# Causal attention in blocks of 256 queries instead of 512, taken from the longest to the shortest, with one exponential over four heads

## The reference

```
scores = (q @ k.T) * 16 ** -0.5            # 1536 x 1536, keys after the query masked out
probs  = exp(scores - max(scores)) / sum    # over the keys
ctx    = probs @ v                          # 1536 x 16
```

## Time and profile before

| | us |
|---|---|
| median of 3 runs (5064.18 to 5069.74) | 5069.07 |
| the profiled execution | 5058.97 |
| its span, first to last instruction | 5056.8 |
| busy: TensorE | 4046.9 (80%) |
| busy: VectorE | 2799.3 (55%) |
| busy: ScalarE | 2255.8 (45%) |
| busy: GpSimd | 494.5 (10%) |
| mean granted clock of TensorE | 0.882 |

### The profile page before, as it was taken

How to read it: one execution, slowest core, us unless ns; L and a number is a source line. 1 busy time by engine, 2 the same in 40 slices (tenths; PEclk the granted TensorE clock), 3 DMA queues, 4 the chain that set the end, 5 groups by cost and what they waited for, 6 DMA issues and landing times. The chain is left out here.

```text
span 5056.8 us, 70418 instructions
## 1 busy us (share of the span) xinstructions
PE 4046.9 (80%) x26656; PEld 2691.9 (53%) x26656; DVE 2799.3 (55%) x6139; ACT 2255.8 (45%) x3803; POOL 494.5 (10%) x824
## 2 busy tenths in 40 slices
PE   6786866799887876799887775799887876799888
PEld 4664644465546544365546554365546554365546
DVE  4555737355555738355555648455545747455544
ACT  3343648254342548254342558254342549244332
POOL 0000010201100010201100010201100010201100
PEclk9898977899898987899898887899898987899988
DMA  2000000000000000000000000000000000000000
GB/s 89 3 3 17 1 17 1 1 1 1 1 1 4 1 17 1 0 1 1 1 1 4 1 18 1 0 1 1 1 1 4 1 1 1 1 1 1 1 1 4
DMA packets 28313, 26.52 MB, mean 5 GB/s; under 512 B 10550, under 2 KB 26934, under 8 KB 27450
## 3 DMA queue, kind: packets, MB, share of 16 engines
q1 hardware_dynamic: 27962, 21.98, 1.5%
HBM read 20.40 MB, written 1.57 MB: 4 GB/s over the span
## 5 line engine op out<-in xcount | busy, mean ns | idle before, releaser
L720 ACT ACTIVATE big<-ps,negmax 128x1024 f32<-128x1024 f32 (+1 forms) x672 | 600.1, 899 | 266.1 <-DVE negmax L753 266.0
L706 ACT COPY big<-ps 128x512 f32<-128x512 f32 x672 | 394.1, 586 | 493.2 <-PE ps L647 490.1
L753 DVE TENSOR_REDUCE negmax<-ps 128x1 f32<-128x1536 f32 x336 | 589.9, 1758 | 38.2 <-PE ps L623 18.5
L647 PE MATMUL ps<-cst,big 128*128 128x128 f32 x4032 | 502.7, 275 | 30.4 <-ACT big L720 29.9
L647 PEld LDWEIGHTS ps<-cst,big 128*128 128x128 f32 x4032 | 457.2, 142 | 48.5 <-ACT big L720 40.5
L424 PE MATMUL ps<-cst 128*128 128x512 f32 x608 | 310.0, 666 | 128.4 <-DVEq L190 58.2
L437 ACT COPY xt<-ps 64x512 f32<-64x512 f32 x144 | 78.9, 579 | 710.7 <-PE ps L429 710.6
L616 PE MATMUL ps<-kup,qup 128*128 128x512 f32 (+3 forms) x768 | 359.2, 565 | 41.8 <-POOLq L190 41.0
L409 POOL TENSOR_TENSOR st<-st,cst 128x6 f32<-128x6 f32 x104 | 156.8, 1508 | 2187.1 <-DVE st L397 2183.0
L663 PE MATMUL ps<-big,v 128*32 128x128 f32 (+1 forms) x8064 | 321.9, 277 | 8.1 <-DVE ctxt L1244 6.0
L616 PE MATMUL ps<-klo,qlo 128*128 128x512 f32 (+3 forms) x672 | 313.7, 550 | 3.6 <-DVE big L706 1.6
(11 more groups left out here) (394 smaller groups left out, 7239.0 us busy)
## 6 DMA issues: line engine op xcount, KB each, us to landing
rw<-in_w_route SPq DMA_DIRECT2D x128, 64.5 KB, 1.8
cst<-in_consts SPq DMA_DIRECT2D x1, 2671.0 KB, 14.6
cst<-in_consts SPq DMA_DIRECT2D x1, 2670.5 KB, 8.7
big<-in_consts SPq DMA_DIRECT2D x1, 1872.5 KB, 21.7
out_dram<-res SPq DMA_DIRECT2D x4, 384.0 KB, 2.9
experts_in<-in_consts SPq DMA_DIRECT2D x1, 1360.0 KB, 17.4
qup<-in_patches SPq DMA_DIRECT2D x4, 260.0 KB
klo<-in_pe_low SPq DMA_DIRECT2D x2, 384.0 KB, 23.1
```

What stands on the lines that cost most here:

```text
L647: ins = nc.tensor.transpose(turned_bank(kind, u, g)[:, i * P:(i + 1) * P], prob[:, slot_of(kind, u), (4 * g + i) * P:(4 * g + i + 1) * P], ...
L706: copy(pt[:, slot_of(kind, u), g, 0:n], turned_bank(kind, u, g)[:, 0:n]).then_inc(*ph.mark(copier(kind, g)))
L720: nc.scalar.activation(prob[:, slot_of(kind, u), cols], src[:, cols], ACT.Exp, bias=bias, accum_out=part_sum[:, u, k:k + 1]).then_inc(*ph. ...
L753: nc.vector.tensor_reduce(negmax[:, u:u + 1], flat[:, 0:n], AX.X, ALU.max, negate=True)\
```

## The change

The blocks become 256 queries (two tiles), and there are six, in the order `seq4` = 5, 4, 3, 2, 1, 0, so the first has 12 steps and the last 2. `cross` now does all four heads of a key tile in one go, four matmuls of 256 columns into two banks, each followed by its edge, and one exponential takes all four (four buffers of `weight` as before, each now one step). The two opening parts of the block after next come before the shifts of the next (`first_parts`); these parts, the shifts and the shift rows are taken before the last exponential and the last two value steps of a block, and the last value step, the copy of the sums and the turn back go into the next block. The shift rows are all copied by ScalarE, four of 256; `keep_clock` goes from four to two. Bank 4 is split: shifts in one half, turned sums in the other. `sums` has two halves by turns.

```diff
-        def steps4(jb):
-            return 4 * (jb + 1)
+        seq4 = (5, 4, 3, 2, 1, 0)
+        half4 = 2 * P
+        def steps4(p):
+            return 2 * (seq4[p] + 1)
...
+            def cross(p, kt):
...
+                edge = kt >= 2 * seq4[p]
+                for hd in range(HEADS):
+                    at = half4 * (hd % 2) + off
+                    bank = ps[:, 2 * (m % 2) + hd // 2, :]
+                    ins = nc.tensor.matmul(bank[:, at:at + half4 - off], k4(hd // 2)[:, kt * P:(kt + 1) * P].bitcast(F32R),
+                                           q4(hd)[:, half4 * seq4[p] + off:half4 * (seq4[p] + 1)].bitcast(F32R),
+                                           start=True, stop=not edge, skip_group_check=True)
+                    if edge:
+                        ins = nc.tensor.matmul(bank[:, at:at + P], future_b[:, :], ident_b[:, :], start=False, stop=True,
+                                               skip_group_check=True)
...
             for i in range(len(parts4(0))):
                 part(0, i)
-            keep_clock(7, 4)
+            keep_clock(7, 2)
+            first_parts(1)
             shifts(0)
...
+            for p in range(len(seq4)):
+                rest = len(parts4(p + 1)) - 2 if p + 1 < len(seq4) else 0
+                for kt in range(steps4(p)):
+                    cross(p, kt)
+                    begin, end = 2 + rest * kt // steps4(p), 2 + rest * (kt + 1) // steps4(p)
+                    middle = (begin + end) // 2
+                    for i in range(begin, middle):
+                        part(p + 1, i)
+                    if kt == steps4(p) - 1 and p + 1 < len(seq4):
+                        for i in range(middle, end):
+                            part(p + 1, i)
+                        first_parts(p + 2)
+                        shifts(p + 1)
                     if kt > 0:
-                        weigh(jb, kt - 1)
...
+                        weigh(p, kt - 1)
+                    elif p > 0:
+                        weigh(p - 1, steps4(p - 1) - 1)
+                    if kt == 1 and p > 0:
+                        turn_back(p - 1)
...
+            def shift_rows(p):
+                act.wait_ge(*ph.after("shift_psum", p + 1))
+                for hd in range(HEADS):
+                    nc.scalar.copy(q4(hd)[64:66, half4 * seq4[p]:half4 * (seq4[p] + 1)].bitcast(F32R),
+                                   ps[32 * hd:32 * hd + 2, 4, 0:half4]).then_inc(*ph.mark("shift_by_act"))
...
+            for p in range(len(seq4)):
+                for kt in range(steps4(p)):
+                    if kt == steps4(p) - 1 and p + 1 < len(seq4):
+                        shift_rows(p + 1)
...
-                for hd in (2, 3):
-                    nc.vector.tensor_copy(q4(hd)[64:66, 512 * jb:512 * (jb + 1)].bitcast(F32R), ps[32 * hd:32 * hd + 2, 4, :])\
-                        .then_inc(*ph.mark("shift_by_vec"))
```

More of the change, by code:

```diff
@@ L1094, in part, with shifts @@
                 ins.then_inc(*ph.mark("part_ready"))
[L1096 to L1111 removed]
+            def shifts(p):
+                pe.wait_ge(*ph.after("shift_ready", p + 1))
+                if p >= 1:
+                    pe.wait_ge(*ph.after("shift_by_act", HEADS * p))
+                for i in range(2):
+                    ins = nc.tensor.matmul(ps[:, 4, i * P:(i + 1) * P], shift[:, i, :], ident, start=True, stop=True,
+                                           skip_group_check=True)
+                ins.then_inc(*ph.mark("shift_psum"))
@@ L1112, in cross @@
+            def cross(p, kt):
+                m = cross_before(p) + kt
+                off = reach(p, kt)
+                if kt == 0:
+                    pe.wait_ge(*ph.after("shift_by_act", HEADS * (p + 1)))
                 if m >= 2:
                     pe.wait_ge(*ph.after("cross_done", m - 1))
-                edge = kt >= 4 * jb
-                for i in range(2):
-                    bank = ps[:, 2 * (m % 2) + i, :]
-                    ins = nc.tensor.matmul(bank[:, off:512], k4(g)[:, kt * P:(kt + 1) * P].bitcast(F32R),
-                                           q4(2 * g + i)[:, 512 * jb + off:512 * (jb + 1)].bitcast(F32R),
-                                           start=True, stop=not edge, skip_group_check=True)
@@ L1120, in cross @@
-                for i in range(2 if edge else 0):
-                    bank = ps[:, 2 * (m % 2) + i, :]
-                    ins = nc.tensor.matmul(bank[:, off:off + P], future_b[:, :], ident_b[:, :], start=False, stop=True,
-                                           skip_group_check=True)
-                ins.then_inc(*ph.mark("cross_psum"))
-            def weigh(jb, kt):
-                m = cross_before(jb) + 2 * kt
-                off = reach(jb, kt)
-                if kt == 0 and jb >= 1:
-                    pe.wait_ge(*ph.after("sums_copied", jb))
-                pe.wait_ge(*ph.after("cross_done", m + 2))
-                for hd in range(HEADS):
-                    ins = nc.tensor.matmul(ps[32 * hd:32 * hd + 32, 7, off:512], v4[:, kt, hd // 2, :],
-                                           weight[:, 2 * (m % 4) + hd, off:512], start=(kt == 0), stop=(kt == steps4(jb) - 1))
-                if kt == steps4(jb) - 1:
-                    ins.then_inc(*ph.mark("sums_ready"))
@@ new lines, in cross, with weigh @@
+                ins.then_inc(*ph.mark("cross_psum"))
+            def weigh(p, kt):
+                m = cross_before(p) + kt
+                off = reach(p, kt)
+                if kt == 0 and p >= 1:
+                    pe.wait_ge(*ph.after("sums_copied", p))
+                pe.wait_ge(*ph.after("cross_done", m + 1))
+                for hd in range(HEADS):
+                    ins = nc.tensor.matmul(ps[32 * hd:32 * hd + 32, 7, off:half4], v4[:, kt, hd // 2, :],
+                                           weight[:, m % 4, hd, off:half4], start=(kt == 0), stop=(kt == steps4(p) - 1),
+                                           skip_group_check=True)
+                if kt == steps4(p) - 1:
+                    ins.then_inc(*ph.mark("sums_ready"))
@@ new lines, in causal_pe @@
+            for p in range(len(seq4)):
[11 more added lines that the diff above has]
+                        shifts(p + 1)
+                    if kt > 0:
+                        weigh(p, kt - 1)
[3 more added lines that the diff above has]
+                        turn_back(p - 1)
+                    if kt < steps4(p) - 1:
+                        for i in range(middle, end):
+                            part(p + 1, i)
@@ L1213, in give @@
                     .then_inc(*ph.mark("ctx_written"))
-            for jb in range(NB):
-                for i, (hd, q, lo, hi) in enumerate(parts4(jb)):
-                    n = parts_before(jb) + i
+            for p in range(len(seq4)):
+                if p >= 1:
+                    dve.wait_ge(*ph.own("shift_ready"))
+                for i, (hd, q, lo, hi) in enumerate(parts4(p)):
+                    if i == 7 and p >= 2:
+                        give(p - 2)
+                    n = parts_before(p) + i
```

154 lines of the change are left out of this document (62 added, 92 removed).

## The result

| | before | after |
|---|---|---|
| median, same chip | 5064.18 us (5058.28 to 5069.74, 5 runs) | 5038.31 us (5035.99 to 5044.68, 5 runs) |
| ratio, 95% interval | | 0.995 (0.9936 to 0.9965) |
| the profiled execution, its span | 5058.97, 5056.8 | 5044.68, 5042.9 |
| mean granted clock | 0.882 | 0.886 |
| attention phase, four passes | 472.25 | 467.94 |

The forecast was 5083 us, slower; the kernel came out faster, by a half per cent. The time lies inside the range of 5035 to 5118, at its lower edge, and on the other side of no change. A second session gave 5049.04 us against 5068.11, 0.9965 (0.9952 to 0.9979). The table already holds the question of the study: of the 13.9 us between the two spans only 4.3 lie in the phase that was changed.

A forecast was written before the change was run, and what follows sets the result against it. TensorE limits the last block, its two-bank PSUM handshake with VectorE costs time in earlier ones. Terms sum to 121.7 us per pass, 486.8 for four against 472.25: 14 more on the 5069.07 median, 5083 us, range 5035 to 5118.

The forecast's parts named there:

- Opening, first score at 24.5: Start of each pass: opening maxima, keep-clock, shifts and four copies put the first score at 24.5 us, against 17.8 before.
- Block ends, "2.3 us idle at each end, 11.7": At the five block ends TensorE was to stand idle 2.3 us each, 11.7 us per pass.
- Work of steps, parts, edges, shifts and end, 80.9: TensorE's work per pass: steps 46.4 and 6.0, edges 5.5, parts 15.5, shifts and turn-backs 6.0, end 1.5 us.
- Clock behind the block ends, 4.6: Inside the blocks, 14 us more at 1.2 GHz, priced at 0.33 us per us: 4.6 us per pass.
- The base: Attention phase of the kernel before, from one profiled execution: 472.25 us over four passes.
- "The change can win or lose only there": Nothing outside the four attention passes is touched, so any gain or loss must lie in their 472.25 us.
- Clock holds: Rival, chance 0.19: clock stays up in the blocks, opening maxima run at VectorE's pace; pass 114.5 us, total 5055.
- Gaps are covered: Rival, chance 0.14: tile switch or load in each step hides under a neighbouring part; 45 us off, total 5038.
- Copies and clock worse: Rival, chance 0.20: ScalarE's shift-row copies cost 0.585 us whatever their width; total 5104, with the clock down 5120.
- the copies at 0.36: Sign: each 256-wide shift-row copy on ScalarE takes 0.36 us.
- TensorE hardly waiting inside the blocks: Sign: in the steps of the longest block TensorE hardly waits for VectorE.
- the 1.7 to 1.9: Sign: steps of the longest block take 1.7 to 1.9 us each.

The follow-up runs named there:

- e10: The changed kernel without the two maxima of the block after next computed ahead of the shifts: 5109.99 us, 1.0095 of the kernel before.
- e11: The kernel before with two 512-column placeholder products at each of its two block ends: 5073.83 us, 1.0026 of the kernel before.

## Why the prediction was wrong

**The sum, term by term.** It gave 121.7 us per pass; the mean of 16 passes is 116.75.

- *Opening, first score at 24.5.* It comes at 23.7. The last maximum ends 18.87 us after the start (18.8 forecast), the clock is down as assumed, the four copies take 1.5 (1.45 forecast). Right; 0.8 too long.
- *Block ends, "2.3 us idle at each end, 11.7".* **This is the step that failed**, with the clock behind it. In the second pass TensorE waits ahead of the early parts 0.52, 0.47, 0.59 and 0.60 (the last end has none), before the shifts 0.31, 0.23, 0, 0 and 1.46, and before the scores 1.04 five times: 9.4 in all, 2.3 less, with 1.6 to 1.9 at the first four ends and 2.5 at the last. Without the early parts the same waits are 13.1 (e10: 8.2 before the shifts and 4.9 before the scores). So the text listed the early parts among what fills the hole, and priced the hole at about the middle between having them and not.
- *Work of steps, parts, edges, shifts and end, 80.9.* From the first score to the end a short pass takes 114.0 - 23.7 = 90.3; less the 9.4 of waits that is 80.9, as forecast. Some of that is luck: the step with two wide parts was overpriced (1.81 against 1.72), so other terms were short by as much; which ones was not measured apart.
- *Clock behind the block ends, 4.6.* Measured 4.0 in 11 of 16 passes: 2.75.

Together: - 0.8 - 2.3 - 1.85 = - 4.95, and 121.7 - 4.95 is the measured 116.75. Over four passes the sum was 20 us too long, 17 of them from the block ends and the clock behind them.

**The base.** "So that the two between take 117.2 each" was right for that one execution, but it was no typical one. The mean of five profiles is 479.0, 6.75 over it. The forecast was a difference of 14 us against this base. With 20 us from the sum and 7 from the base it becomes the measured - 12. The median of before that it was put on, 5069.07 from three runs, came out 5 lower with five. The remaining 13 of the 45 us between 5083 and 5038 are gain outside what the profiles show of the phase, and their cause stays open. The two pass times stood in the earlier trace rows, 117.25 and 120.60, and served only as a price per microsecond; whether the shares of the two could change from one execution to the next was not asked.

**"The change can win or lose only there"** is neither shown nor refuted: the profiles put 12.0 of 15.2 us in the phase, within a scatter outside it of 14 us that is larger than the effect, and the medians gained 7 to 14 us more than the phase did. One pair of profiles could not have shown a gain of 12 us in the phase: the first pair showed 4.3.

**The rivals.** *Clock holds* had the short pass nearly right, 114.5 against 114.0, but for another reason: the opening maxima did not run at VectorE's pace, and the block ends were cheaper. *Gaps are covered* gave the median (5038) with the wrong mechanism. The load after a value step is still not covered: the value step starts at 2524.75 and the next weight load at 2525.32, 0.57 later, as in the earlier trace rows. That load also had to wait for a maximum, as the one in the earlier trace rows had; the second step of the next block has one that waits for nothing, 0.36 behind the start of a value step of 128 queries:

```profile
2545.45 0.43 PE L1137 MATMUL ps<-big,v 128*32 128x128 f32 x8
...
2545.81 0.19 PEld L1091 LDWEIGHTS ps<-k_stack,q_stack 128*128 128x128 f32 x1 [0.20 <-issue]
```

The Trainium skill, "TensorE: Matmul & The Clock Gate", section "Step-by-step: what each phase is for", has loads pulled ahead of running matmuls when the row groups do not conflict or the load goes to the background buffer. At this switch of tile shape none is pulled ahead in the changed kernel either; which of the two conditions fails no run shows. *Copies and clock worse* falls: a copy of 256 columns takes 0.37 us on ScalarE.

**What was foreseen.** Of the signs listed, the copies at 0.36 and TensorE hardly waiting inside the blocks came true; steps came at 1.48 to 1.72, mostly under the 1.7 to 1.9, and 2.17 where the edges begin; the holes of about 1 us are there (1.04). Signs of error came true too: the phase came out below 117 in the mean, one step at 1.48, and the clock in the blocks above 0.95 in the short passes.

## What to carry to other kernels

A hole on TensorE has two prices, the wait and the clock level of what follows, and the second can be the larger: two early parts of 0.3 to 0.4 us moved into the holes were worth 14 us a pass against a short pass of after, some 11 of them the clock. Before a change of a per cent or less is priced, profile the kernel several times and see whether its stages take one time or two; a base from one execution can be off by half the effect. When hand-over copies stand in one chain on one engine, split the chain first: here that gave more in the phase (6.4 us a pass) than the whole change did (3.0). And count every wait of a block end, those ahead of the filling work too.

## What the hardware did that was not expected

- The same pass of the same kernel takes 114.0 or 118.0 us (before 117.2 or 120.6), and nothing between in the profiles of one kernel apart from a few tenths. Runs of one kernel largely follow their mean granted clock: of 27 runs of before on one chip the fastest, 5058.67 us, has 0.883 and the slowest, 5080.6, has 0.876.
- With stops of 1.46 to 1.87 us before the shifts, followed by 0.75 to 1.05 before the scores (e10), the mean clock was down in each of the blocks that follow (0.92 to 0.60). With the stops of after, 0.47 to 0.60 ahead of the early parts, 0 to 0.31 before the shifts (1.46 before the last) and 1.04 before the scores, it was down nowhere in its second pass and in two places of its first. The last end is the same in both, and its block ran at 0.60, 0.67 or 1.00.
- In e11, whose placeholder matmuls shortened the phase, the stage behind it ran one stretch of matmuls without a hole at 0.50 in two of four batches (17.28 us) and at 1.00 in the others (9.20). No run shows that the placeholders are the reason.
- With four PSUM banks instead of two under the opening maxima the placeholder matmuls behind them ran in 1.94 us instead of 3.23: the opening that keeps VectorE fed also ran at the upper clock level.
